# Decoder layer with routed experts: batch 0's projection ahead of the last value products, routing steps 2 to 7 as a loop, two weight semaphores

## What is computed

```
attn = einsum('nlhs,nshd->nlhd', softmax(q k / sqrt(D)), v)
x = layernorm(x + x + attn @ Wo + bo)
logits = x @ Wr + br;  top 2 of 8;  weights = softmax over the two
for e in range(8):
    h = relu(x @ W1[e] + b1[e]);  y = h @ W2[e] + b2[e]
    out = out + y * weights[e]
x = layernorm(x + out)
```

## Time and profile before

| | us |
|---|---|
| median of three runs (lowest to highest) | 2202.6 (2199.92 to 2205.04) |
| the profiled execution: its time | 2195.98 |
| its span, first to last instruction | 2194.3 |
| PE busy in it | 1981.7 (90%) |
| DVE busy | 1754.2 (80%) |
| ACT busy | 1540.5 (70%) |
| POOL busy | 736.3 (34%) |
| mean granted clock of PE, full speed is 1 | 0.960 |

### The profile page before, as it was taken

The page is one execution under the profiler, slowest core; times in us unless marked ns, Lnnn a source line. Parts: engine busy times, 40 slices in busy tenths (PEclk is TensorE's granted clock), DMA queues, the critical chain, the costliest instruction groups (busy, mean ns, idle before and its releaser), DMA issues.

```text
span 2194.3 us, 43516 instructions
## 1 busy us (share of the span) xinstructions
PE 1981.7 (90%) x10630; PEld 1044.8 (48%) x10638; DVE 1754.2 (80%) x3559; ACT 1540.5 (70%) x4345; POOL 736.3 (34%) x983
## 2 busy tenths in 40 slices
PE   7898998899999999999999998888829999999994
PEld 3554555322322232222322221112729999999994
DVE  5889885799999999999999999998635555555554
ACT  4655565899999999999999999998402333233333
POOL 0112111244444444444444441111563333333333
PEclk9989999999999999999999999999859999999997
DMA  4111105776758576676668576661771222222225
GB/s 156 44 44 72 58 24 130 193 125 116 112 110 145 118 110 117 119 124 135 90 131 136 108 111 92 123 77 42 223 197 32 37 36 37 36 36 36 36 36 168
DMA packets 126117, 212.39 MB, mean 97 GB/s; under 512 B 31554, under 2 KB 94786, under 8 KB 124882
## 3 DMA queue, kind: packets, MB, share of 16 engines
q1 hardware_dynamic: 98272, 151.74, 37.8%
q0 software_dynamic: 26240, 59.00, 10.2%
q10 hardware_dynamic: 1554, 1.05, 0.2%
HBM read 138.38 MB, written 73.74 MB: 97 GB/s over the span
## 4 chain that ended last, share of the span: by engine, by line
PE 39%; ACT 30%; issue 18%; DVE 7%; POOL 3%; DMA 2%; ACTq 1%; DVEq 0%; SPq 0%; POOLq 0%
ACT w_all L1429 26%; PE psum L1715 12%; PE psum L1725 11%; PE psum L473 6%; DVE neg_max L1336 3%; POOL list_all L1595 3%; PE psum L1239 2%; PE psum L1271 2%; ACT w_all L822 1%; PE psum L1702 1%; DMA v_all<-w_all 1%; PE psum L500 1%; ACTq L1428 1%; DVE stats L1016 0%; DVE stats L1995 0%
## 5 line engine op out<-in xcount | busy, mean ns | idle before, releaser
L1429 ACT ACTIVATE w_all<-psum,neg_max 128x512 f32<-128x512 f32 (+1 forms) x1664 | 1111.1, 736 | 18.2 <-DVE neg_max L1336 16.6
L1336 DVE TENSOR_REDUCE neg_max<-psum 128x1 f32<-128x512 f32 (+1 forms) x1664 | 1024.9, 677 | 17.3 <-PE psum L1271 14.2
L1271 PE MATMUL psum<-qst,kst 96*128 96x512 bf16 (+1 forms) x1664 | 527.7, 389 | 73.1 <-ACT w_all L1429 63.1
L1239 PE MATMUL psum<-w_all 128*32 128x512 f32 (+1 forms) x3328 | 448.9, 612 | 9.5 <-DVE w_all L1350 9.3
L1271 PEld LDWEIGHTS psum<-qst,kst 96*128 96x128 bf16 (+1 forms) x1664 | 130.0, 98 | 658.1 <-ACT w_all L1429 639.0
L1769 ACT ACTIVATE hid<-psum,b 128x128 f32<-128x128 f32 x568 | 161.9, 368 | 393.1 <-PE psum L1715 393.1
L1429 ACT ACTIVATION_READ_ACCUMULATOR w_all<-psum,neg_max 128x1 f32 (+1 forms) x1664 | 426.8, 257 | 0.0
L1402 POOL TENSOR_TENSOR w_all<-vst,inv 128x64 f32<-128x64 f32 (+1 forms) x416 | 121.0, 291 | 658.3 <-DVE inv L1304 654.7
L1715 PE MATMUL psum<-xst,w 128*128 128x128 f32 x2272 | 267.4, 277 | 0.0
L1715 PEld LDWEIGHTS psum<-xst,w 128*128 128x128 f32 x2272 | 261.6, 193 | 0.1
L1725 PE MATMUL psum<-area,hid 128*128 128x256 f32 x1136 | 257.0, 380 | 0.0
(11 more groups left out here) (209 smaller groups left out, 1878.1 us busy)
## 6 DMA issues: line engine op xcount, KB each, us to landing
kst<-k_parts SPq DMA_DIRECT2D x384, 112.0 KB, 6.5
k_parts<-k_out POOLq DMA_DIRECT2D x52, 336.0 KB, 3.0
w_all<-in_W SPq DMA_DIRECT2D x16, 1024.0 KB, 11.9
area<-in_ctxT SPq DMA_DIRECT2D x16, 896.0 KB, 4.7
vst<-v_all SPq DMA_DIRECT2D x64, 224.0 KB, 9.2
qst<-q_parts SPq DMA_DIRECT2D x192, 64.0 KB, 5.9
v_all<-area POOLq DMA_DIRECT2D x13, 896.0 KB, 4.3
q_parts<-q_out POOLq DMA_DIRECT2D x24, 256.0 KB, 3.0
```

What stands on the lines that cost most here:

```text
L1239: last = pe.matmul(psum[j * PAD:(j + 1) * PAD, 6, :], v_scaled[0:r, pb, j, :], probs_at[pb][0:r, j, :], start=t == 0, stop=t == ST - 1)
L1271: pe.matmul(psum[0:r, 2 * sbuf + i, :], kst[:, h, j, t * P:t * P + r], qst[:, h, j, :], start=True, stop=True).then_inc(scores_ready, 1)
L1336: v.tensor_reduce(neg_max[0:r, sbuf, i:i + 1], psum[0:r, 2 * sbuf + i], AX_X, ALU.min) \
L1429: act.activation(probs_at[pb][0:r, j, :], psum[0:r, 2 * sbuf + i, :], ACT.Exp, bias=neg_max[0:r, sbuf, i:i + 1], scale=-1.0, accum_out=sum ...
```

## The change

Three parts.

1. **Batch 0.** `project` and `norm_rows` become functions of the whole expert part (`project_rows`, `norm_rows`). In the last round of attention, PE projects batch 0 ahead of the last two value products, once the last exponentials out of banks 0 and 1 are done. DVE sums and norms batch 0 ahead of its copy of the last attention.
2. **Loop.** Steps 0 and 1 stay written out; steps 2 to 7 become a loop of two steps an iteration on DVE and ACT; on PE and SP the loop has steps 2 to 5. POOL's scatters stay written out. Batch numbers in semaphore counts, transfer addresses and in `slot_u` and `pairs` become functions of the loop's variable. PE's `ranks` no longer waits for `slots_ready`.
3. **Weights.** `ffn_loaded` becomes `w1_loaded` and `w2_loaded`. For tile 0, DVE copies the bias and the first weight before it reads the lists, and the second weight after it has taken the rows.

```
@@ attend_tensor, tile_step
+                    if tile == N_TILE + 1 and is_over(tile, it):
+                        pe.wait_ge(xwo_loaded, 16)
+                        pe.wait_ge(exp_done, 2 * N_SUB * it + 2 * LAST_OF_FIRST + 2 + 2 * CREDIT)
+                        project_rows(pe, 0, 0, 1, range(TT))
                     if tile >= LAG:
                         pv(tile - LAG, it)
@@ attend_vector, tile_step
+                    if tile == N_TILE + LAG - 1 and is_over(tile, it):
+                        v.wait_ge(v_scaled_ready, N_TILE * (it + 1))
+                        norm_rows(v, 0, 0)
                     for h in range(2):
                         if tile == ST * (h + 1) + LAG - 1:
@@ load_route
+        def load_route(sp, b, h):
+            one = bass.ds(b, 1)
+            sp.dma_start(at_in[:, h], attn_all.rearrange("(b c g) j d l -> b (g j d) c l", b=B, c=C)[one]
+                         .rearrange("o p c l -> (o p) c l")).then_inc(route_loaded[h], 16)
+            sp.dma_start(x1_in[:, h].rearrange("p t d -> p (t d)"), x1_all[one].rearrange("o p f -> (o p) f")) \
                 .then_inc(route_loaded[h], 16)
@@ the steps
+            def route_steps(eng, step, turns, last):
+                def one(c, it, h, like):
+                    step(c, it, h, like < B, 0 <= like - 1 < B, 0 <= like - 2 < B)
+                for c in range(2):
+                    one(c, 0, c, c)
+                with eng.Fori(1, turns) as it:
+                    for h in range(2):
+                        one(2 * it + h, it, h, 2 + h)
+                for c in range(2 * turns, last):
+                    one(c, c // 2, c % 2, c)
@@ experts_sync, experts_tensor, experts_scalar, experts_vector
-                for c in range(B):
-                    route_step(c)
+                route_steps(sp, route_step, B // 2 - 1, B)
-                pe.wait_ge(xwo_loaded, 16)
-                project(0, range(TT))
-                for c in range(B + 2):
-                    route_step(c)
+                route_steps(pe, route_step, B // 2 - 1, B + 2)
-                for c in range(B + 1):
-                    route_step(c)
+                route_steps(act, route_step, B // 2, B + 1)
-                for c in range(B + 2):
-                    route_step(c)
+                route_steps(v, route_step, B // 2, B + 2)
@@ experts_tensor, ranks
-                    wait(pe, slots_ready, s)
@@ experts_vector, ahead of the tiles
-                for d in range(3):
-                    name_rows(d, 16)
-                v.wait_ge(ffn_loaded, 32 * E)
-                at = copy_weights(slice(0, 1), 0)
-                v.wait_ge(xs_t_ready, 1)
-                take_rows(0)
-                v.wait_ge(b2_loaded, 16)
-                scale_bias(at, 0)
+                v.wait_ge(w1_loaded, 16 * E)
                 v.wait_ge(x2_ready, B)
                 for h in range(2):
                     v.wait_ge(x2_stored[h], 16 * B)
+                at = copy_first(slice(0, 1), 0)
+                for d in range(3):
+                    name_rows(d, 16)
+                v.wait_ge(xs_t_ready, 1)
+                take_rows(0)
+                v.wait_ge(w2_loaded, 16 * E)
+                copy_second(at, 0)
+                v.wait_ge(b2_loaded, 16)
+                scale_bias(at, 0)
                 tiles(v, tile_step)
```

More of the change, by code:

```diff
@@ L1135, in decoder_layer @@
             CREDIT = N_TILE
+            LAST_OF_FIRST = max(k for k in range(N_SUB) if score_buf[k] == 0)
             def free(k, buffer_of, it):
@@ L1540, in decoder_layer, with wide, project_rows @@
             assert TILES % DESTS == 3 and TT * D == HID and B >= 4
+            def wide(t):
+                return t.rearrange("p t d -> p (t d)").rearrange("p (n f) -> p n f", n=2)
+            def project_rows(pe, b, h, loads, ts):
+                if ts[0] == 0:
+                    wait(pe, y2_ready, b - 1)
+                    pe.wait_ge(route_loaded[h], 32 * loads)
+                for t in ts:
+                    at = psum[:, 2 * h + t // 2, (t % 2) * D:(t % 2 + 1) * D]
+                    for k in range(C):
+                        last = pe.matmul(at, at_in[:, h, k, t * P:(t + 1) * P], xwo[:, k, :], start=k == 0,
+                                         stop=k == C - 1)
+                if ts[-1] == TT - 1:
+                    last.then_inc(proj_ready, 1)
@@ new lines, in norm_rows @@
+            def norm_rows(v, c, h):
+                norms = Steps(NORM_STEPS * c)
+                wait(v, x2_ready, c)
+                v.wait_ge(proj_ready, c + 1)
+                v.tensor_tensor(wide(y2), psum[:, 2 * h:2 * h + 2], wide(x1_in[:, h]), ALU.add) \
+                    .then_inc(y2_ready, 1)
+                v.wait_ge(y2_ready, c + 1)
+                for t in range(TT):
+                    v.bn_stats(stats2[:, t], y2[:, t]).then_inc(dve_norm, 1)
+                    s = norms.next()
+                wait_alone(v, (dve_norm, s))
+                for t in range(TT):
+                    last = v.bn_aggr(moments2[:, t], stats2[:, t])
+                last.then_inc(moments2_ready, 1)
@@ L1542, in experts_sync, with route_step @@
             def experts_sync(sp):
-                def route_step(c):
-                    h = c % 2
-                    if c < B and c + 2 < B:
+                def route_step(c, it, h, norm, choose, place):
+                    if not (isinstance(c, int) and c + 2 >= B):
                         sp.wait_ge(y2_ready, c + 1)
[L1547 to L1552, removed]
+                        load_route(sp, c + 2, h)
+                    sp.wait_ge(x2_ready, c + 1)
+                    for rows_to in (sums_all, x2_rows):
+                        sp.dma_start(rows_to[0:TOKENS].rearrange("(b p t) d -> b p t d", b=B, t=TT)[bass.ds(c, 1)]
+                                     .rearrange("o p t d -> (o p) t d"), x2[:, h]).then_inc(x2_stored[h], 16)
@@ L1643, in experts_tensor, with turn @@
             def experts_tensor(pe):
[L1644 to L1658, removed]
+                def turn(e, h):
                     wait(pe, x2t_copied, e)
@@ L1684, in ranks, with route_step @@
                               start=True, stop=True).then_inc(ranks_ready, 1)
[L1686 to L1691 removed]
+                def route_step(c, it, h, norm, choose, place):
+                    more = not (isinstance(c, int) and c + 1 >= B)
+                    if choose:
+                        turn(c - 1, 1 - h)
+                    if more:
+                        project_rows(pe, c + 1, 1 - h, it + h + 1, (0, 1))
+                    if place:
                         ranks(c - 2)
[L1693 removed]
+                    if choose:
                         route(c - 1)
[L1695 to L1696 removed]
+                    if more:
+                        project_rows(pe, c + 1, 1 - h, it + h + 1, (2, 3))
                 def take(half, count):
```

94 lines of the change are left out of this document (33 added, 61 removed).

## The result

| | before | after |
|---|---|---|
| median of 17 runs each, side by side (us) | 2201.32 (2195.46 to 2209.51) | 2211.71 (2206.3 to 2216.19) |
| the profiled execution: its time | 2195.98 | 2211.71 |
| its span | 2194.3 | 2210.0 |
| mean granted clock of PE | 0.960 | 0.957 |

The changed kernel is slower: ratio 1.0042, 95% interval 1.0033 to 1.0051, or 10.4 us between the medians. The two profiled executions are 15.7 us apart; the one of before lies 5.3 us under its median, so they overstate the loss by that much. The loss lies between the end of attention and the first expert tile: that tile starts at 1662.58 instead of 1647.9, 14.7 us later, and the 71 tiles behind it cost about 1 us more.

The account below looks back on a forecast made before the run. POOL's scatters were taken as the bound: when the first starts and what follows the last. Terms: +6.6 us at the list loads, -1.4 us tail, sum +5.2; 2207.8 against median 2202.6, range 2197.5 to 2215.

Parts of the forecast that it names:

- likeliest case: End of attention to first expert tile: late route load, idle PE, clock fall; +5.2 us, range 2204.6 to 2211.6, chance 0.38.
- rival 3: Weights become the bound: mid-stage stall comes again, lists wait behind 8 MB; +11.4 us, 2214; chance 0.17.
- Batch 0 earlier: End of attention: batch 0's projection ahead of two value products, so its sum starts 2.2 us earlier.
- The copy 4.7 us later: DVE's last attention copy, now behind batch 0's norm: at 1532.8 instead of 1528.13.
- Route load landed at 1543.1: Batch 2's route load: W1 issue at 1535.3 plus 7.8 us to landing; its projection starts 4.2 us later.
- The clock: PE, idle 5.9 us before batch 2's projection, then runs at half clock: 6.3 us, bounds 0 and 8.1.
- The loop: Register operations in routing steps: 0.5 us before the first slots, later covered by POOL; back edges cost nothing.
- rival 4: Loop back edges stall on instruction fetches on DVE, TensorE and ACT: up to +10 us, near 2212; chance 0.06.
- The mid-stage interval: Long interval between x2 stores (13.3 against 7.4 us) should go, leaving the last x2 store +5 us.
- List loads: Ahead of expert tile 0: last scatters land by some 1644.5 instead of 1637.9, +6.6 us.
- The tail: Expert tile 0: weights copied before lists are read; -1.4 us, between 0 and 2.4.
- four things that I had said would prove me wrong: Batch 2's projection follows the turn at once; first scatter earlier; POOL waits later; list loads long after last scatter.

Follow-up runs that it names:

- route load first: Changed kernel with SP issuing batch 2's route load ahead of its wait for the last attention copy; ratio to before 1.0019, again 1.0018.
- copy first: Changed kernel with DVE's last attention copy put back ahead of batch 0's norm, PE's new order kept; ratio to before 1.0029.
- W1 last of all: Changed kernel with the last W1 load issued ahead of the last x2 store; ratio to before 1.0034.
- kernel before with W1 moved: Kernel before with only the last W1 load moved behind SP's second x2 store; 2209.6 us, ratio to before 1.0019.
- mended kernel: Changed kernel, batch 2's route load ahead of the copy wait, last W1 load behind second x2 store; to before 0.9998 with loop, 0.9989 and 0.9998 without.

## Why the prediction was right in sign and short in size

The sign, the mechanism and its place were right: slower, through SP's queue behind the late attention copy, an idle PE before batch 2's projection, and the clock behind it. The time, 2211.7 against 2207.8, lies in the range, but just above the likeliest case's own range (2204.6 to 2211.6), toward rival 3. The measured 10.4 us are twice the 5.2 forecast, and nearer to rival 3's 11.4.

- **Batch 0 earlier** by 2.2 us: right where the clock stays up. In the four traces with the sum at 3.4 (the route load first, with and without W1 moved) it is 2.1 us earlier than before (5.5). In the trace after, PE ran at 0.51 from 1524.40 to 1527.80, two value products took 3.04 instead of 1.85 us and the projection 4.25 instead of 3.6: 0.4 was left. Two kernels that keep the old order there show the same fall (sum at 6.8), so the early projection is not what brings it.
- **The copy 4.7 us later**: in the traces without that fall it is at 6.5 against 1.8, 4.7 us; in the trace after 6.3. But I laid it to the norm ahead of it on DVE, and most of it is PE's order: with the copy first again it still came at 6.9, behind the last value products. With the same fall of the clock it is at 3.1 in the old order, 6.9 with PE's new order and 8.1 with DVE's too, so 3.8 of the 5.0 us are PE's.
- **Route load landed at 1543.1**: it was 1545.9. This was the step that failed in the first half. 1.3 us came from the sum's late start. The rest is the term of 7.8 us from the W1 issue to the landing, which measured 9.3. Without W1 ahead the second half landed 6.0 us behind its issue instead of 7.6, still more than the 4.8 of before, where W1 was ahead. So something else slowed it too, likely the x2 stores of batches 0 and 1 and the load of batch 3, all issued within 6 us behind it; that was not tried by itself. My words "with the DMA engines full" were too strong: their share was 0.73 from 1530 to 1539.
- **The clock**: 6.3 us predicted; half projection, routing, half projection and turn took 3.75, 3.42, 3.76 and 1.91 instead of 1.89, 1.85, 1.97 and 1.09, which is 6.0 us. That this one fits is in part luck, since the same kind of wait had very different prices behind it: 1.9 us after 6.06 idle (W1 last of all), 6.0 after 4.56 (copy first) and after 7.61, 1.5 after 3.91 (route load first). My 6.3 came from a single fall. For the first scatter +10.3 was predicted and +12.5 measured: batch 2's projection started 2.9 us later than I had it, and 0.7 came back behind it.
- **The loop**: +0.5 predicted, 0.0 measured from sum to first scatter in the kernel with the loop alone. Steps were 7.8 to 8.7 us apart where no load was waited for, under POOL's 10.2, so POOL never waited, as predicted. Back edges: POOL, which is what a stall would have to reach, was fed throughout, and the page of the profile counts fewer instruction packets after than before (22 and 29 before), not more for every turn:

```profile
q8 instruction: 21, 0.34, 0.1%
q14 instruction: 27, 0.22, 0.0%
```

  By the rule of the Trainium skill that I cited ("Runtime: NRT & Kernel Launch", instruction fetch mechanics) each taken branch to a target outside the two pages held would fetch one. These counts and the 19.2 us show no such stall, and rival 4 falls. The rule itself is not tested: I had taken it to hold for each back edge, but no run shows whether a target lay outside those pages. And the loop has three turns on DVE and ACT and two on PE, so they went back twice and once, not two or three times.
- **The mid-stage interval "should go"**: this was the larger error. It came again, 11.7 us from the sum of batch 6 to that of batch 7, around the wait of 2.90 us at 1593.26, so the last x2 store was 10.4 us later, not 5. That a stall had been taken at the start did not make the transfers any less dense later on. Rival 3 had this, with near 13.
- **List loads**: +6.6 predicted, +16.2 measured. Of the 9.6 between them, 5.4 is the later start of the stream. The rest is the stream itself: from the first W2 issue to the list loads it took 45.4 us against 39.7. I had the last scatters landing just behind it (and they did: bias landed at 1653.95, list loads at 1655.05), but let the 8 MB take as long as before. In the other traces with W2 alone in it this stretch took 38.6 to 44.8 us, without an order that I could find (44.8 in the kernel before with W1 moved, 39.8 and 38.7 in the mended one), so part of the 16.2 belongs to this one trace; the medians, 10.4 us apart, hold less of it. What sets the stream's length was not settled.
- **The tail**: -1.4 predicted; from list loads to tile 0's product 7.5 us against 9.0, and 7.7 with this part alone.

Of the four things that I had said would prove me wrong, one came: list loads long behind the last scatter (10.3 us, before 7.3). The right reading is the likeliest case's first half with rival 3's second half.

## What to carry to other kernels

When a step is moved ahead of another on one engine, follow the displaced step to the queue that waits for it, and list every transfer behind it: here 2 us won on DVE made a 0.5 MB load 5 us later, and it stood in front of the critical engine. Issue the load that the next step needs ahead of waits and of bulk loads that nobody needs yet; and when a bulk load is moved, look at whose load comes behind it in the new place: here, with the DMA engines 83 to 90% busy between 1541 and 1580 us of the kernel before, W1 stood in front of batch 3's load in one place (3.91 us of waiting) and of batch 4's in the next (4.24 and 2.98). An idle stretch of TensorE costs its length and then again something through the clock. In these traces that was 1.4 to 6.0 us after waits of 2.9 to 7.6 us, not in the order of the waits, so give it a range and not a fixed multiple. And read every kernel's trace as far as the step that ends the stage: 5 us won at the first scatter were gone at the last one.

## What the runs showed of the hardware that was not expected

**The same kernels differ by 16 to 20 us between sets, each on another chip, through stalls in the routing stage.** The kernel before took 2221.63, 2223.99 and 2223.07 us on three chips and 2204.07 on a fourth (2201.32 in the first comparison). In every trace of the first three, at least one and mostly two or three times in the routing stage, DVE stands 9 to 16 us in front of the router's logits, though by PE's records their matmuls were through; POOL's scatters go on until they run out, and the DMA engines move next to nothing. The mended kernel without the loop on the one chip, around such a stall (timeline, then stretches by time):

```profile
1563.20 1.93 PE L1715 MATMUL psum<-router_w,w 128*128 128x8 f32 x16
...
1576.30 0.19 DVE L1881 TENSOR_TENSOR logits<-psum,router_b 128x32 f32<-128x32 f32 x1 [11.01 <-remote]
```

```profile
1567.00:1575.00 8.00, 2.79 (x16) 2.27 (x16) 0.00 (x0) 0.48 (x1) 6.17 (x7) 0.89 0.40 132
1575.00:1580.00 5.00, 0.88 (x4) 0.88 (x4) 2.62 (x19) 0.84 (x2) 1.15 (x2) 0.50 0.04 2
```

The same kernel on the fourth chip, the same stretches:

```profile
1567.00:1575.00 8.00, 8.00 (x30) 7.02 (x31) 4.79 (x24) 3.31 (x6) 6.04 (x7) 0.59 0.66 137
1575.00:1580.00 5.00, 4.43 (x31) 3.83 (x29) 3.96 (x37) 2.67 (x7) 3.49 (x4) 1.00 0.70 209
```

It took 2220.33 us on the one and 2204.38 on the other; its last scatter was issued 127.9 and 105.6 us behind the last exponential. In the kernel before it was 127.6 on a chip with stalls and 105.3 without, 22.3 us apart, near the 18 to 23 us between the medians. (Those two profiled executions are 30.9 us apart; 3.2 of them lie ahead of the last exponential, 5.1 between the last scatter and tile 0.) Most of the stalls end within 1 to 4 us of scatter 16, 32, 40 or 48, the last one for which slots were ready. They come with and without the loop and in every version, so a ratio compares like with like, but they may hide or repay a few us of a late first scatter. Their cause is open: no experiment went at it, and whether they belong to the chip or to the time of the set is not shown either.

**The clock falls or does not in the same attention code.** In the last value products the granted clock was 0.51 for 3.4 us in the trace after and 1.00 throughout in that of before. The two mended kernels have the same code there and differ only in the steps behind it, as a loop or written out: the one fell, the other did not. Of 14 traces seven show the fall, with the old order on PE and with the new. It moves the sum of batch 0 by 1.3 to 1.7 us, most of what the change was to win there. Whether it is chance is not shown: the three kernels that were traced twice did the same both times.
